# Attention on one core: key sums in three running chains, products with V in bursts of two tiles, and the scaling of o in the last stage

## What is computed

```python
x = x + attn(layernorm(x))
x = x + ffn(layernorm(x))
# attn
q = x @ Wq.T + bq + ocr_bias; k = x @ Wk.T + bk; v = x @ Wv.T + bv
scores = einsum("bhsd,bhtd->bhst", q, k) / sqrt(32) + band     # band: 0.1 where |s - t| <= 2
out = einsum("bhst,bhtd->bhsd", softmax(scores), v)
return out @ Wo.T + bo
# ffn
return dequantised(x) @ dequantised(weight).T + bias
```

## Time and profile before

| | us |
|---|---|
| median of 3 runs | 4577.78 (4577.1 to 4581.52) |
| the profiled execution | 4576.01 |
| its span, first to last instruction | 4574.1 |
| PE busy | 4436.7 (97%) |
| DVE busy | 3378.5 (74%) |
| ACT busy | 2446.5 (53%) |
| POOL busy | 2828.9 (62%) |

### The profile page before, as it was taken

The page is one execution under the profiler, slowest core; times in us unless marked ns, Lnnn a source line. Parts: engine busy times, 40 slices in busy tenths (PEclk is TensorE's granted clock), DMA queues, the critical chain, the costliest instruction groups (busy, mean ns, idle before and its releaser), DMA issues. The chain is left out here.

```text
span 4574.1 us, 62800 instructions
## 1 busy us (share of the span) xinstructions
PE 4436.7 (97%) x22928; PEld 2504.6 (55%) x22928; DVE 3378.5 (74%) x5663; ACT 2446.5 (53%) x4652; POOL 2828.9 (62%) x927
## 2 busy tenths in 40 slices
PE   7999989999999999999999999999999999977999
PEld 6888845454445444444445454444454444525777
DVE  5444467888888888788787888888888788735776
ACT  2222216666666666666666666666666666651121
POOL 2111017778878787787877778878787787870000
PEclk9999969999999999999999999999999999988999
DMA  7666545555565656565656555565656565445452
GB/s 253 206 212 205 197 120 118 129 124 131 125 140 117 140 113 145 110 144 121 142 118 132 128 124 131 125 140 117 140 113 144 112 144 117 104 89 199 147 178 108
DMA packets 287700, 640.71 MB, mean 140 GB/s; under 512 B 40641, under 2 KB 107201, under 8 KB 249538
## 3 DMA queue, kind: packets, MB, share of 16 engines
...
## 5 line engine op out<-in xcount | busy, mean ns | idle before, releaser
L702 DVE TENSOR_REDUCE part_max<-ps_m 128x1 f32<-128x512 f32 x4096 | 2548.9, 683 | 654.0 <-PE ps_m L598 650.5
L772 POOL TENSOR_TENSOR pair<-p_sb 128x2048 f32<-128x2048 f32 x512 | 2348.4, 4587 | 665.5 <-ACT p_sb L690 301.9
L690 ACT ACTIVATE p_sb<-ps_s 128x512 f32<-128x512 f32 x4096 | 2114.8, 602 | 1130.3 <-PE ps_s L618 1129.8
L618 PE MATMUL ps_s<-q_st,k_st 97*128 97x512 f32 x4096 | 1732.4, 425 | 17.1 <-ACT p_sb L690 17.1
L598 PE MATMUL ps_m<-k_st,q_st 96*128 96x512 f32 x4096 | 1646.0, 405 | 42.0 <-POOL k_st L765 20.1
L618 PEld LDWEIGHTS ps_s<-q_st,k_st 97*128 97x128 f32 x4096 | 774.0, 189 | 1031.4 <-ACT p_sb L690 619.3
L632 PE MATMUL ps_o<-p_sb,v_sb 128*32 128x512 f32 x8192 | 1092.4, 605 | 0.2 <-DVE p_sb L729 0.2
L598 PEld LDWEIGHTS ps_m<-k_st,q_st 96*128 96x128 f32 x4096 | 785.7, 192 | 230.6 <-DVE part_max L702 76.3
L632 PEld LDWEIGHTS ps_o<-p_sb,v_sb 128*32 128x32 f32 x8192 | 161.3, 108 | 345.2 <-ACT p_sb L690 289.3
L166 POOL TENSOR_TENSOR xb<-xin,bo_row 128x2048 f32<-128x2048 f32 x16 | 75.3, 4706 | 424.7 <-DMA xin<-in_x 414.0
L642 PE MATMUL ps_d<-pair,ones 128*32 128x512 f32 x2048 | 267.5, 594 | 9.9 <-DMA pair<-pair 9.9
...
## 6 DMA issues: line engine op xcount, KB each, us to landing
pair<-pair POOLq DMA_DIRECT2D x256, 1024.0 KB, 7.3
q_st<-q_hi_d SPq DMA_DIRECT2D x128, 256.0 KB, 4.2
k_st<-k_hi_d SPq DMA_DIRECT2D x128, 256.0 KB, 5.5
xin<-in_x SPq DMA_DIRECT2D x16, 1024.0 KB, 8.2
xb_d<-xb SPq DMA_DIRECT2D x16, 1024.0 KB, 5.2
...
```

The lines of the kernel that those rows point to most:

```text
L618: nc.tensor.matmul(ps_s[:, (HG * s + h) % RING_S, :], k_st[0:ROWS + 1, unit // QC % 2, kt // TT, h, kt % TT * P:(kt % TT + 1) * P], q_st[0 ...
L690: nc.scalar.activation(p_sb[:, s % SLOTS, h, :], ps_s[:, (HG * s + h) % RING_S, :], ACT.Exp, scale=SCALE).then_inc(p_ready, 1)
L702: nc.vector.tensor_reduce(part_max[:, unit % 2, col, n:n + 1], ps_m[:, seq % RING_M, :], AX.X, ALU.max).then_inc(max_taken, 1)
L772: nc.gpsimd.tensor_tensor(pair[:, m % PAIR_RING], p_sb[:, s % SLOTS], p_sb[:, (s + 1) % SLOTS], ALU.add).then_inc(paired, 1)
```

## The change

**Products with V.** `weigh` is issued only at even s, for the two tiles s-2 and s-1 in one burst. The maxima's ring gets a fourth bank; the sums no longer have a bank of their own and take a place in that ring once per unit.

**Exponentials.** `p_sb` and `pair` go. Tiles of even steps lie in `p_even` (eight, one for each pair of a unit), those of odd steps in `p_odd` (ring of four). POOL adds the odd tile into the even one in place, and so waits until both were weighed (`pv_done`).

**Key sums.** The eight sums of pairs of a unit form three chains: for pairs 3 to 7 a DMA adds pair n-3 to pair n. Five DMAs of 1 MB per unit take the place of four, and PE sums three tiles instead of four, all at step kt = 6 of the next unit.

**Band.** `spread_band(s - 1)` stands behind the second of the four maxima of step s, where before two of them stood together between pairs of steps.

**o.** `attend` stores o unscaled, once. The sums are inverted once per set of four units. `finish` loads o and the inverses, multiplies, and splits: chunk 0 on DVE, the others on POOL with ACT making the high part (8 POOL and 4 ACT instructions of 128x512 for each chunk).

The diff, cut to its core:

```diff
+def keys_of(part_d, g):
+
+    return part_d[QC * g:QC * (g + 1)].rearrange("u h t -> (u h t)").rearrange("(p n) -> p n", p=P)
...
-    RING_S, RING_M = 3, 3
+    RING_S, RING_M = 3, 4
     MAXES = HG * TT * QC
     TURN_AFTER = 8
-    SLOTS = 8
     PAIRS = KT // 2
-    QUADS = PAIRS // 2
-    SUM_LAG = 9
-    PAIR_RING = 4
-    NDEN = HG * CH // P
+    ODD = 4
+    CHAINS = 3
+    MERGES = [(PAIRS - 1 - c) // CHAINS for c in range(CHAINS)]
+    SUM_AT = 6
+    SUM_AFTER = HG * (SUM_AT + LEAD + 1)
...
+    def sums_before(unit, j):
+
+
+        return max(unit - 2 + (j >= SUM_AFTER), 0)
...
+    def sum_place(unit):
+        return max_place(unit + 2, SUM_AFTER) - 1 if unit < NU - 2 else MAXES * NU + NU + unit
...
+    def merges_to(m):
+
+        return MERGES[m % PAIRS % CHAINS] * (m // PAIRS) + m % PAIRS // CHAINS
...
-        p_sb = sb("p_sb", [P, SLOTS, HG, CH])
-        pair = sb("pair", [P, PAIR_RING, HG, CH])
+        p_even, p_odd = sb("p_even", [P, PAIRS, HG, CH]), sb("p_odd", [P, ODD, HG, CH])
         ones = sb("ones", [P, HD])
-        o_lo, o_hi = sb("o_lo", [P, CH], F32R), sb("o_hi", [P, CH], F32R)
-        o_st, sum_st, rec_b = f32(o_lo[:]), f32(o_hi[:]), f32(o_hi[:])
+        o_st, sum_st = sb("o_st", [P, CH]), sb("sum_st", [P, CH])
...
+        def p_of(s):
+            return p_odd[:, s // 2 % ODD] if s % 2 else p_even[:, s // 2 % PAIRS]
...
             def store_o(unit):
-                sp.wait_ge(o_split, unit + 1)
-                sp.dma_start(o_hi_d[unit], f32(o_hi[:])).then_inc(o_out, 16)
-                sp.dma_start(o_lo_d[unit], f32(o_lo[:])).then_inc(o_out, 16)
+                sp.wait_ge(o_copied, unit + 1)
+                sp.dma_start(o_d[unit], o_st[:]).then_inc(o_out, 16)
 
...
+            def free_bank(place):
+
+                old = place - RING_M
+                if old in sum_places:
+                    pe.wait_ge(sum_copied, sum_places[old] + 1)
+                else:
+                    at_least(pe, max_taken, old + 1 - sums_to[max(old, 0)])
+                return place % RING_M
...
-            def add_keys(quad):
-                unit, n = quad // QUADS, quad % QUADS
-                if n == 0:
-                    at_least(pe, sum_copied, unit)
-                pe.wait_ge(merged[quad % 2], 16 * (quad // 2 + 1))
-                for h in range(HG):
-                    last = nc.tensor.matmul(ps_d[h * HD:(h + 1) * HD, :], ones[:], pair[:, 2 * quad % PAIR_RING, h, :],
-                                            start=(n == 0), stop=(n == QUADS - 1))
+            def add_keys(unit):
+                bank = free_bank(sum_place(unit))
+                for m in range(PAIRS - CHAINS, PAIRS):
+                    pe.wait_ge(merged[m % CHAINS], 16 * MERGES[m % CHAINS] * (unit + 1))
+                    for h in range(HG):
+                        last = nc.tensor.matmul(ps_m[h * HD:(h + 1) * HD, bank, :], ones[:], p_even[:, m, h, :],
+                                                start=(m == PAIRS - CHAINS), stop=(m == PAIRS - 1))
                 last.then_inc(sum_done, 1)
 
...
-            for s in range(ST + SUM_LAG - 3):
+            for s in range(ST + SUM_AT + 1):
                 if s < ST:
                     for h in range(HG):
                         score(s, h)
                         ahead(*max_at(s, h))
-                if 2 <= s < ST + 2:
+                if s % 2 == 0 and 2 <= s < ST + 2:
                     weigh(s - 2)
-                if s >= SUM_LAG and s % 4 == SUM_LAG % 4:
-                    add_keys((s - SUM_LAG) // 4)
+                    weigh(s - 1)
+                if s >= KT and s % KT == SUM_AT:
+                    add_keys(s // KT - 1)
 
         @block.scalar
...
-                if s >= SLOTS:
-                    act.wait_ge(pv_done, s - SLOTS + 1)
-                    act.wait_ge(paired, (s - SLOTS) // 2 + 1)
+                m = s // 2
+                if s % 2 and m >= ODD:
+                    act.wait_ge(pv_done, s - 2 * ODD + 1)
+                    act.wait_ge(paired, m - ODD + 1)
+                if s % 2 == 0 and m >= PAIRS:
+                    if m % PAIRS < PAIRS - CHAINS:
+                        act.wait_ge(merged[m % PAIRS % CHAINS], 16 * merges_to(m - PAIRS + CHAINS))
+                    else:
+                        act.wait_ge(sum_done, unit)
...
             for m in range(NM):
-                if m > 0:
-                    spread_band(2 * m - 1)
                 for s in (2 * m, 2 * m + 1):
                     for h in range(HG):
                         ahead(*max_at(s, h))
-                spread_band(2 * m)
-                if m % PAIRS == 4 and m > PAIRS:
-                    invert(m // PAIRS - 1)
+                        if h == 1 and s > 0:
+                            spread_band(s - 1)
+                if m % (QC * PAIRS) == 6 and m > PAIRS:
+                    invert(m // (QC * PAIRS) - 1)
...
                     pool.wait_ge(banded, bands_to[s + 1])
-                at_least(pool, sum_done, (m - PAIR_RING) // 2 + 1)
-                nc.gpsimd.tensor_tensor(pair[:, m % PAIR_RING], p_sb[:, s % SLOTS], p_sb[:, (s + 1) % SLOTS],
-                                        ALU.add).then_inc(paired, 1)
-                if m % 2 == 1:
+                pool.wait_ge(pv_done, s + 1)
+                nc.gpsimd.tensor_tensor(p_of(s), p_of(s), p_of(s + 1), ALU.add).then_inc(paired, 1)
+                n = m % PAIRS
+                if n >= CHAINS:
+                    at_least(pool, merged[n % CHAINS], 16 * (merges_to(m) - 1))
                     pool.wait_ge(paired, m + 1)
-                    pool.dma_start(pair[:, (m - 1) % PAIR_RING], pair[:, m % PAIR_RING],
-                                   accum_op=ALU.add).then_inc(merged[m // 2 % 2], 16)
-                if m % PAIRS == 5 and m > PAIRS:
...
+                    pool.dma_start(p_of(s), p_of(s - 2 * CHAINS), accum_op=ALU.add).then_inc(merged[n % CHAINS], 16)
...
             def load_o(c):
-                at_least(sp, out_projected, TT * (c - 1))
-                sp.dma_start(f32(o_hi[:, c % 2]), o_by_chunk(o_hi_d, c)).then_inc(o_in[c % 2], 16)
-                sp.dma_start(f32(o_lo[:, c % 2]), o_by_chunk(o_lo_d, c)).then_inc(o_in[c % 2], 16)
+                at_least(sp, o_split, NHG * (c - 1))
+                sp.dma_start(o_raw[:, c % 2], o_by_chunk[c]).then_inc(o_in[c % 2], 16)
+                if c == NCH - QC:
+                    sp.wait_ge(rec_last, 16)
+                for g in range(NHG):
+                    sp.dma_start(o_rec[:, c % 2, g, :],
...
+            for c in range(1, NCH):
+                b = c % 2
+                if c == 1:
+                    pool.wait_ge(o_split, NHG)
+                pool.wait_ge(o_in[b], 16 * (c // 2 + 1))
+                pool.wait_ge(rec_in[b], 16 * NHG * (c // 2 + 1))
+                for g in range(NHG):
+                    nc.gpsimd.tensor_tensor(o_raw[:, b, g, :], o_raw[:, b, g, :], o_rec[:, b, g, :],
+                                            ALU.mult).then_inc(o_scaled, 1)
+                for g in range(NHG):
+                    pool.wait_ge(o_high, NHG * c + g + 1)
+                    nc.gpsimd.tensor_tensor(o_lo[:, b, g, :], o_raw[:, b, g, :], f32(o_hi[:, b, g, :]),
+                                            ALU.subtract).then_inc(o_split, 1)
...
+            def o_highs(c):
+                at_least(act, out_projected, TT * (c - 1))
+                for g in range(NHG):
+                    act.wait_ge(o_scaled, NHG * c + g + 1)
+                    nc.scalar.activation(o_hi[:, c % 2, g, :], o_raw[:, c % 2, g, :], ACT.Copy).then_inc(o_high, 1)
...
+                        if t == 0:
+                            pe.wait_ge(o_split, NHG * c + k + 1)
```

162 lines of the change are left out of this document (79 added, 83 removed).

## The result

| | before | after |
|---|---|---|
| median, us | 4578.35 (beside the runs of after) | 4901.29 (4895.42 to 4907.99, 4 runs) |
| ratio to before | | 1.0704 [1.0688, 1.072] |
| profiled execution, its span | 4576.01, 4574.1 | 4895.42, 4893.6 |
| first to last shift row, by 63: one unit | 53.53 | 57.31 |
| last shift row made to the end | 539.6 | 624.4 |

The table splits the loss. The 64 units cost 3.8 us more each, some 240 in all, where 582 were forecast. The rest of the program, from the last shift row on, costs 85 us, where 8 were to be gained.

What follows compares the result with a forecast made beforehand. PE's instruction order bounds the kernel; a unit of 49.9 + 9.1 (band) + 0.6 (shift row) + 3.0 (clock) = 62.6 us, +9.1 on 53.5, so 64 x 9.1 less 8 on 4576.0 gives 5150 us; range 4930 to 5340.

Steps and rivals of the forecast that it cites:

- Unit without its band: In attend, a unit with no band cost: 46.6 + 2.6 + 0.3 + 0.3 = 49.9 us, 3.6 below 53.5.
- Plain run: In attend, two steps with one double burst and no band: 5.83 us on PE instead of 6.14.
- The chain of arrivals at DVE, ACT and POOL: In attend, these engines follow a run of sixteen; only ACT's copy of o costs, 0.3 us a unit.
- The hold: In attend, DVE's two-SBUF-input multiplication waits for POOL's addition: +3.6 us a doubly banded run, +2.5 even tile only; 9.1 a unit.
- When POOL starts: In attend, POOL's addition starts with the run and lasts until 4.7 us into it, holding the even tile's multiplication.
- The clock: In attend, PE's idle gaps lower its clock: 1.0 us a gap, 12 per four units, 3.0 us a unit (0 to 5.1).
- Last stage: In finish, the start saves 8 us (-10 to -6); later chunks' loads cost 0 (0 to 42).
- Shift row: At unit ends, its DMA falls behind the merging DMA in u = 2: about 2.5 us, 0.6 a unit.
- the first: Rival for attend: holds occur, but the clock stays up or its loss falls into other waits; 4958 us, chance 0.2.
- The second: Rival for attend: no multiplication is held, +0.9 us a doubly banded run, unit 51.7; 4453 us, chance 0.07.
- The third: Rival at unit ends: shift row also late in units without band at kt 12, +202 us; 5350 us, chance 0.12.
- the fourth: Rival for attend: POOL starts later or half the holds are missed, costs a third; near 4576 us, chance 0.06.

Runs made afterwards that it cites:

- the fills: Changed kernel with POOL's addition replaced by three constant fills that read nothing, key sums left out: 4546.64 us in one execution.
- the bands together: Changed kernel with a pair's two band multiplications side by side again, behind the fourth reduction of a run: 4515.55 us, ratio 0.9861.
- the loads ahead: Changed kernel with the last stage's loads of o and the inverses issued one chunk earlier: 4845.09 us, ratio 1.0593.

## Why the prediction was right in direction and 249 us too high

- **Unit without its band: 49.9 forecast, 49.7 measured** without the band. Plain run 5.83 and 5.80. The chain of arrivals at DVE, ACT and POOL, worked out from single rows, held.
- **The hold, right.** A multiplication with two inputs in SBUF ends 0.56 us after POOL's addition (0.55 in the earlier trace rows). Write-only POOL work leaves it at 0.69. The odd tile's stays at 0.69, as forecast.
- **When POOL starts, wrong.** This is the step that failed: "Now POOL starts to add the previous pair at the end of the burst, that is with the run, and adds until 4.7 us into it." The wait is for `s + 1`, the even tile. In the run shown POOL started 1.0 us ahead of the run and was through at 3.6. The held multiplication ends some 1.1 us sooner, the even tiles' take 2.07 on the mean (3.3 forecast for the doubly banded run), and PE's gaps are shorter by as much (1.49 in the run shown, forecast 2.6). The kernel with the wait as I had read it takes 61.6 us a unit. So the misreading, with the clock that hangs on it, gave 64 x (61.6 - 57.3) = 275 us too much, and the two runs themselves differ by 272. The forecast stood at 62.6: another 1.0 a unit, 64 us, was too much for that kernel too. One part of it is seen: I let every doubly banded run cost 3.6, but at kt = 7 of u = 1, where the sums stand ahead of the run, POOL starts 2.7 us ahead even there, and the run costs 1.1.
- **The clock, mis-sized with it.** Forecast: 192 gaps of 1.0, 3.0 us a unit. There are 74 stretches of half clock from 700 us to the last shift row, together 297 us; if half of it was lost, 148 us, that is 2.3 a unit at most. In the same part of the kernels whose holds are short or gone they all but vanish (none without the band, none with the fills, one with the bands together). Of the 3.4 us a unit by which PE is busy longer than without the band, the clock can thus explain 2.3 at most; what the rest is, no run settles.
- **Last stage, mis-sized.** Forecast: -8, of bounds -10 to -6 for the start and 0 to 42 for the chunks. Measured: +85. The -8 counted scaling and splitting, and took the loads in front of them to be no slower than before. The way to the first load did shrink, from 16.6 us to 2.2 (4346.02 to 4348.21; "about 4" was forecast, for which no row stood). But from the first load to the first product it took 10.5 us before (4126.16 to 4136.70) and takes 24.6 now (to 4372.78), of which 21.4 go until o's first chunk and its inverses have landed, so nothing was saved (27.4 us of idle against 27.8). The bound of 42 for late loads was the nearer to what came, and taking 0 was the choice that erred; the loads took some 59 of the 85 (624.4 to 565.3), as their repair shows. Of the other 26, 7 are idle time of PE and 18 are longer busy time. That a later stage with new gaps also runs at a lower clock was in no term. Chunk 1's wait alone is 13.7 with the loads ahead, and others became shorter, as that for the first transposes (6.8 before, 3.5).
- **Shift row, right in kind:** 26.9 us of wait for 64 units (0.4 a unit, forecast 0.6; the forecast's own times, 12.3 less 10.2, give 2.1 us and not 2.5). 22.9 of it stand behind units with u = 2, where it was forecast.

As a sum: 5150, less 275 (POOL's start, with the clock that hangs on it), less 64 (what was too much even with the wait as read), plus 93 (last stage: +85 instead of -8), gives 4904; measured 4901. The sum closes by its making, since units and tail are read from the same trace; what is tested is the 275. It is luck, too, that the attention's error of -339 was partly made up by the last stage's +93.

The rivals: the first, in which the clock stays up, was the nearest in time (4958), but not in kind: the clock does fall, at fewer places. The second, nothing held, is what the fills showed (a unit of 51.6, forecast 51.7; its 4453 plus the tail's 93 is 4546, measured 4547). The third, a shift row that comes late in the units without a band at kt = 12, did not come: behind those units PE waits 0.2 us for it in all. Nor did the fourth, in which POOL starts later; it started earlier.
